# Spreading reciprocal softmax sums over the rows of a result: by a buffer off the chip in place of products with a selection matrix

## The reference, cut to what matters

```python
q = (x @ wq).reshape(b, n, heads, dh).transpose(0, 2, 1, 3)   # heads 20, dh 8
k = (ctx @ wk).reshape(b, j, heads, dh).transpose(0, 2, 1, 3)
v = (ctx @ wv).reshape(b, j, heads, dh).transpose(0, 2, 1, 3)
sim = jnp.einsum('bhid,bhjd->bhij', q, k) * dh ** (-0.5)
a = jax.nn.softmax(sim, axis=-1)
out = jnp.einsum('bhij,bhjd->bhid', a, v)
return out.transpose(0, 2, 1, 3).reshape(b, n, heads * dh) @ wo + bo
```

## Time and profile before

| | us |
|---|---|
| median of 3 runs | 3791.29 |
| lowest and highest run | 3786.4, 3798.77 |
| the profiled execution: its own time | 3797.55 |
| its span, first to last instruction | 3795.8 |
| mean granted TensorE clock over the span | 0.97 |
| PE busy in the span | 3625.6 (96%) |
| VectorE busy | 2304.9 (61%) |
| ScalarE busy | 2093.5 (55%) |
| GpSimd busy | 1249.9 (33%) |

### The profile page before, as it was taken

The page is one execution under the profiler, slowest core; times in us unless marked ns, Lnnn a source line. Parts: engine busy times, 40 slices in busy tenths (PEclk is TensorE's granted clock), DMA queues, the critical chain, the costliest instruction groups (busy, mean ns, idle before and its releaser), DMA issues. The chain is left out here.

```text
span 3795.8 us, 98161 instructions
## 1 busy us (share of the span) xinstructions
PE 3625.6 (96%) x37907; PEld 3133.8 (83%) x37907; DVE 2304.9 (61%) x3920; ACT 2093.5 (55%) x5164; POOL 1249.9 (33%) x1275
## 2 busy tenths in 40 slices
PE   5999999997997999999999999699999999999899
PEld 4777778876886888888898888588888888888788
DVE  2788866662454566666666666455555655556454
ACT  2777777773433655555555555355555555554333
POOL 4333333321442233333333332222222322222442
PEclk8999999995998999999999999899999999999899
DMA  4343333321001000000000000100000000000000
GB/s 109 90 102 101 92 82 91 87 77 50 5 0 44 1 1 0 0 0 0 0 0 0 0 0 1 25 3 2 2 2 1 2 2 2 2 1 1 16 21 24
DMA packets 99546, 98.72 MB, mean 26 GB/s; under 512 B 31248, under 2 KB 74128, under 8 KB 99344
## 3 DMA queue, kind: packets, MB, share of 16 engines
q1 hardware_dynamic: 94224, 94.50, 9.4%
q0 software_dynamic: 5120, 1.35, 0.2%
HBM read 20.76 MB, written 5.24 MB: 7 GB/s over the span
## 5 line engine op out<-in xcount | busy, mean ns | idle before, releaser
L1137 POOL TENSOR_TENSOR a_probs<-a_probs,a_rsums 128x1024 f32<-128x1024 f32 x160 | 303.6, 1898 | 750.6 <-DVE a_rsums L1235 750.6
L1157 ACT ACTIVATE a_probs<-a_scores_banks,a_negmax 128x128 f32<-128x128 f32 x1280 | 366.6, 376 | 297.6 <-DVE a_negmax L1223 297.6
L1137 POOL TENSOR_TENSOR c_probs<-c_probs,c_rsums 128x616 f32<-128x616 f32 x160 | 201.2, 1258 | 767.8 <-DVE c_rsums L1235 767.8
L702 ACT ACTIVATE s_probs<-s_scoresT_banks 128x1024 f32<-128x1024 f32 (+1 forms) x320 | 327.1, 1022 | 205.0 <-PE s_scoresT_banks L860 203.0
L1157 ACT ACTIVATE c_probs<-c_scores_banks,c_negmax 128x77 f32<-128x77 f32 x1280 | 312.1, 334 | 203.8 <-DVE c_negmax L1223 203.8
L777 DVE TENSOR_REDUCE s_negmax<-s_scores_banks 128x8 f32<-128x1024 f32 (+1 forms) x320 | 322.4, 1007 | 153.4 <-PE s_scores_banks L842 149.3
L1216 DVE COPY c_outT<-c_out_bank 128x512 f32<-128x512 f32 x160 | 110.7, 692 | 368.9 <-PE c_out_bank L1377 308.6
L1216 DVE COPY a_outT<-a_out_bank 128x512 f32<-128x512 f32 x160 | 110.7, 692 | 296.1 <-PE a_out_bank L1377 244.1
L1521 DVE SCALAR_TENSOR_TENSOR f_hidden<-f_value_bank,bias,f_gate 128x512 f32<-128x512 f32 x160 | 120.2, 751 | 263.1 <-ACT f_gate L1498 261.1
L665 POOL DMA_DIRECT2D s_q_stack<-s_shift x160 | 93.4, 584 | 523.3 <-ACT s_shift L725 517.4
L1498 ACT ACTIVATE f_gate<-f_gate_bank,bias 128x512 f32<-128x512 f32 x160 | 109.9, 687 | 257.3 <-PE f_value_bank L323 257.3
(11 more groups left out here) (288 smaller groups left out, 10613.9 us busy)
## 6 DMA issues: line engine op xcount, KB each, us to landing
s_q_stack<-s_q_compact SPq DMA_DIRECT2D x192, 160.0 KB, 3.2
s_k_stack<-s_k_compact SPq DMA_DIRECT2D x96, 160.0 KB, 3.6
s_out<-s_heads SPq DMA_DIRECT2D x128, 80.0 KB, 2.2
s_k_stack<-s_k_compact SPq DMA_DIRECT2D x96, 96.2 KB, 2.8
x_tokens<-in_x SPq DMA_DIRECT2D x16, 320.0 KB, 5.1
out_x<-x_tokens SPq DMA_DIRECT2D x16, 320.0 KB, 2.4
s_q_stack<-s_shift POOLq DMA_DIRECT2D x160, 8.0 KB, 2.5
s_ctx_in<-in_ctx SPq DMA_DIRECT2D x16, 115.5 KB
```

The source lines that it names most:

```text
L702: nc.scalar.activation(probs[i][0:NK, :, :], scoresT[0:NK, :, :], ACT.Exp).then_inc(s_exp, 1)
L1137: nc.gpsimd.tensor_tensor(probs[i][:], probs[i][:], rsums[(k - 1) % 2][:].unsqueeze(2).broadcast_to([P, UNIT, NK]), ALU.mult).then_inc(s_p ...
L1157: done = nc.scalar.activation(probs[i][:, h, :], scores[:, h // GROUP, h % GROUP * NK:(h % GROUP + 1) * NK], ACT.Exp, bias=negmax[k % 2][: ...
```

## The change

`select` and its products are gone. In unit 9 of period `n + 1` SyncE writes the reciprocal sums to a buffer in memory off the chip (`sums_out`, 40 KB). In unit 0 of period `n + 2` it waits until that has landed and reads them back by four transfers of 80 KB, each row of the buffer eight times, into `spread`, a tile of the shape of `out`. `sums` is now a part of `spread`, so the load of the next sums waits for the multiplies. VectorE multiplies the two halves of `out` by `spread` in two following units (`sums_at` now names units 2 and 3 in place of 1 and 3, and the multiply comes one unit behind), after a wait for all four transfers. PE's waits for `max_bank` between maxima and spread sums are gone.

```diff
-        sums = sb("sums", [HALF, P])
+        sums_out = nc.dram_tensor(f"{tag}_sums_out", (HALF * P,), F32, kind="Internal").ap()
+        spread = sb("spread", [HALF, 2, QUAD * P])
+        sums = spread[:, 0, 0:P]
...
-            return ((s - 1) // 2, n) if s in (1, 3) and live(n, TOTAL) else None
+            return (s - 2, n) if s in (2, 3) and live(n, TOTAL) else None
...
+                if s == 9 and live(prev, TOTAL):
+                    sp.wait_ge(s_rsums, prev + 1)
+                    sp.dma_start(sums_out.rearrange("(p n) -> p n", n=P), sums).then_inc(s_sums_out, 16)
+                if s == 0 and live(prev - 1, TOTAL):
+                    sp.wait_ge(s_sums_out, 16 * prev)
+                    if due(2 * (prev - 1)):
+                        sp.wait_ge(s_out, 2 * (prev - 1))
+                    for b in range(2):
+                        for j in range(2):
+                            source = sums_out[(2 * b + j) * 20 * P:(2 * b + j + 1) * 20 * P]
+                            sp.dma_start(spread[40 * j:40 * (j + 1), :, b * 2 * P:(b + 1) * 2 * P],
+                                         source.rearrange("(a g n) -> a g n", a=1, g=GROUPS).broadcast_to([8, GROUPS, 4 * P]))\
+                                .then_inc(s_spread, 16)
                 if s == 6 and live(prev, TOTAL):
                     sp.wait_ge(s_heads, GROUPS * (prev + 1))
-                    sp.dma_start(sums[:], heads[(local - 1) % 2][1:P:32, :, :]).then_inc(s_sums_in, 16)
+                    if due(prev):
+                        sp.wait_ge(s_out, 2 * prev)
+                    sp.dma_start(sums, heads[(local - 1) % 2][1:P:32, :, :]).then_inc(s_sums_in, 16)
...
-                spread = sums_at(k - 1)
-                if spread:
-                    half, n = spread
-                    dve.wait_ge(s_spread, 2 * n + half + 1)
+                scaled = sums_at(k - 1)
+                if scaled:
+                    half, n = scaled
                     if half == 0:
                         dve.wait_ge(s_out_in, 16 * OUT_DMAS * (n + 1))
-                    nc.vector.tensor_tensor(out[:, half, :], out[:, half, :], max_bank[0:HALF, :], ALU.mult).then_inc(s_out, 1)
+                        dve.wait_ge(s_spread, 16 * 4 * (n + 1))
+                    nc.vector.tensor_tensor(out[:, half, :], out[:, half, :], spread[:, half, :], ALU.mult).then_inc(s_out, 1)
...
-                    if g in (0, 1) and due(n - 1):
-                        pe.wait_ge(s_out, 2 * (n - 2) + g + 1)
...
-                spread = sums_at(k)
-                if spread:
-                    half, n = spread
-                    pe.wait_ge(s_rsums, n + 1)
-                    pe.wait_ge(s_shift, upto(5 * (n + 2) + half + 1 - 1, 5 * TOTAL))
-                    if n + 2 >= TOTAL:
-                        pe.wait_ge(s_out, 2 * n + half)
-                    for b in range(2):
-                        for r in range(2):
-                            col = (2 * b + r) * P
-                            last = nc.tensor.matmul(max_bank[0:HALF, col:col + P], m.select[0:HALF, b, 2 * half + r, :], sums[:],
-                                                    start=True, stop=True)
-                    last.then_inc(s_spread, 1)
...
-                link(nc.gpsimd.memset(m.select[:], 0.0))
-                for b in range(2):
-                    for x in range(4):
-                        place = m.select[0:D // 2, b, x, :].rearrange("p (j d g) -> p j d g", j=2, g=GROUPS)
-                        link(nc.gpsimd.affine_select(out=place, in_=place, compare_op=ALU.not_equal, fill=1.0, base=-(40 * b + x),
-                                                     pattern=[[-20, 2], [0, 8], [-4, GROUPS]], channel_multiplier=1))
```

More of the change, by code:

```diff
@@ L541, in attention_small @@
         s_rsums = sem("rsums_ready")
+        s_sums_out = sem("rsums_out")
         s_spread = sem("rsums_spread")
@@ L797, in step @@
                     dve.wait_ge(s_sums_in, 16 * quad_of(k))
-                    nc.vector.reciprocal(sums[:], sums[:]).then_inc(s_rsums, 1)
+                    nc.vector.reciprocal(sums, sums).then_inc(s_rsums, 1)
                 if s == 7 and live(ahead, TOTAL):
@@ L1594, in build @@
         m.minus_half = sb("minus_half", [P, QUAD])
-        m.select = sb("select", [P, 2, 4, D // 2])
         m.minus_low_row = sb("minus_low_row", [P, 1])
```

## The result

The changed kernel took 4066.15 us (median of 4 runs, 4050.41 to 4085.16), the kernel before 3789.06 in the same comparison (3786.40 to 3798.77): ratio 1.0728, 95% interval 1.0672 to 1.0784. The forecast was 3748, and the range ended at 3792. The profiled execution took 4075.63 us, against the 3797.55 shown of before.

A forecast was written before the change was run, and what follows sets the result against it. PE order was taken to set the time, VectorE following closely. Gains of 14.6 us in self, 21.1 in cross and 7.0 in the remaining periods made 43 us, from a median of 3791.29 to 3748; range 3730 to 3792.

The forecast's parts named there:

- The clock stays, as counted: End of the forecast's sum: 43 us gained, 3748 us, with the granted clock unchanged.
- PE has no idle time in those units without the sets either: Argument against the clock falling in cross quads, where two of ten units have sets but no unread products.
- its sum for cross: Cross quads: unit 5 starts at +10.62 against +12.13, gaining 1.51 us in each of 14, 21.1 us.
- The price of a fall: Quads at half clock: about 33 to 35 us instead of 25.25, 9 us more each, 45 us in all.
- up to five quads until a burst: Cross: a clock fall lasts at most until a burst in quads 18, 23 or 28, costing 45 us.
- The rival that the clock falls: Cross quads: without the sets PE works less and the clock drops; 3793 to 3835 us; chance 7%.
- The chain: SyncE's write, wait, four reads and VectorE's wait per quad: 6.0 us, bounds 5.5 to 7.6, worst 10.0.
- the rival of late transfers: Chain over about 8 us delays VectorE and PE; 3819 at 10.0 us; 10% slower, 20% for 7 to 9 us.
- the gain of undisturbed quads: Quads whose transfers land early: 1.38 us gained in self, 1.51 us in cross.
- the lock: Multiply from two SBUF tiles waits out GpSimd's running operation, then takes 0.57 us; rival without it 3731, 13%.
- the start, hidden as before: Kernel start: removing nine GpSimd operations on `select` changes nothing, as GpSimd idles 19.92 us afterwards.
- the signs of what to watch: Signs of error included VectorE idle 1 us or more before multiply 0 and clock 0.50 before 840 us.

The follow-up runs named there:

- run 5: Run 1 with GpSimd's shift transfer of unit 2 issued ahead of L422 and L424; 3765.41 us, ratio 0.9936.
- run 1: The changed kernel without the write and four reads, spread set once to 1.0, normalisation by the sums mostly left out; 3981.08 us.
- run 9: The changed kernel with GpSimd's shift transfer of unit 2 ahead of L422 and L424, both multiplies later in VectorE's unit 4; 3763.58 us, ratio 0.9927.
- run 10: Run 9 with reciprocal, write and reads early, in unit 8; 3755.00 us, ratio 0.9890.
- run 6: The changed kernel with reciprocal, write and reads early in unit 8, and GpSimd's shift transfer of unit 2 ahead of L422 and L424; 3881.73 us.
- run 4: The changed kernel with the reciprocal, write and reads moved early, into unit 8; 3985.64 us.
- run 11: Run 10 with four products that nobody reads per unit in quad 2 too; 3764.84 us, from 3745.30 to 4007.89 in five runs.
- run 2: The changed kernel with four unread products put back in units 1 and 3, ahead of the projection; 3819.04 us (3786.70 to 4063.57).
- run 7: The changed kernel with only GpSimd's shift transfer of unit 2 moved ahead of L422 and L424; 4021.05 us.
- run 8: The kernel before the change with 1.6 us of unread GpSimd work between L424 and the shift transfer of unit 2; 3873.31 us, ratio 1.0170.

## Why the prediction was wrong

**The step that failed** is the last sentence of the sum, "The clock stays, as counted", and the argument under its rival: "PE has no idle time in those units without the sets either". It took TensorE's order alone as the pace, and looked for what comes late only along the new chain. With the sets gone TensorE comes sooner to everything else that it waits for, and one of these, GpSimd's shift transfer behind the normalisation, had 4.1 us of cover in cross and then 2.1. The prediction had both ends of it in its sum for cross: L424 pushed to +9.25, and unit 5 at +10.62 (measured +10.49). Its scores take 0.64, so by these numbers the transfer behind L424 has 10.62 + 0.64 - 9.25 = 2.0 us, which it didn't set against the landings. In the kernel before, 8 of the 28 landings at this place, 5 of the 14 in cross, took more than 2.1 us from their issue (2.3 to 3.4); none made TensorE wait. Its trace had all of this, issue, landing and the use.

**The price of a fall** was wrong as well. A cross quad at half clock was put at 33 to 35 us from 102 records in 8 us, a stretch of longer products. It took 41.4 (44.0 in every fifth), 16 us more a quad and not 9. And "up to five quads until a burst" was no bound: of three bursts of fills at half clock one (in quad 23) was followed by a rise, and that held for 31 us. Of the fifteen periods that lost 221 us, twelve lost 15 to 17 each, 195 together. The rival that the clock falls, given 7%, had the end of the mechanism right, but the wrong beginning, missing work, which run 5 refutes for cross.

**The chain** took 6.0 us in the sum, within 5.5 to 7.6, with 10.0 as the worst. In the quads where VectorE waited it took 6.7 to 8.8. The write landed sooner than the 2.2 taken (1.5 at the median); the four reads were issued in 2.92 us, 0.73 each where at most 0.63 was assumed, and VectorE went on up to 4.1 us after the last issue ended (332.70 - 328.55). SyncE's own lateness was taken as up to 1.15 us, and was up to 2.4. So VectorE waited in 7 of 14 self quads, and in 4 of them TensorE stopped for more than 1 us: the rival of late transfers. Its price, 2.0 us a quad at 10.0, left the clock out: two periods around such a stop took 59.6, 61.3 and 62.8 us against 50.0 before, 10 to 13 us more.

**Right** were: the gain of undisturbed quads (self quads of 23.4 us in run 1, 23.6 in run 5 and 23.75 in the runs 9 and 10, 1.2 to 1.6 less than before, 1.38 forecast; cross 1.4 to 1.6 less, 1.51 forecast); the lock, with multiplies of 1.0 to 1.5 us amid GpSimd's work and 0.68 without; the start, hidden as before; and the signs of what to watch, waits before multiply 0 and the clock at 0.50 before 840 us. The sum, 43 us, is near what the edit is worth when hardly anything stops: run 10, with its new orders, gained 34. That the multiply waits for the whole GpSimd instruction is what the Trainium skill, "SBUF — State Buffer", SBUF: two separate sides, states; the trace agrees, with 1.52 us at 391.59, which ends 0.6 us after L424, and run 6 adds that it can be two instructions.

**Of a wait's size** the runs say this: in self the falls came behind stops of 1.7 to 3.4 us in the changed kernel, while stops of 0.68 us were passed, but in run 4 it fell behind stops of 0.64 and 0.68, at 177 and 330 us; in cross the falls came behind 1.86, 1.16, 1.16, 2.08, twice 2.39, 2.19 and 0.96 us, while 0.85 and 0.59 were passed. Where self passes into cross, stops of 0.5 to 0.6 us were passed in the kernel before and brought it down for 304 us in run 11. What exactly makes it fall is left open, as is why some landings of 8 KB take 1.7 us and others 4.7.

## What to carry to other kernels

When work is taken from the engine that sets the pace, list everything else that this engine waits for, and read for each how long before its use it is ready now: work that is removed was cover for all of them, not only for what replaces it. A transfer's cover has to be measured against its slowest landings (here 4 to 5 us beside a usual 1.8), since each quad draws again. And where the granted clock hangs on an unbroken stream, price a stop by what the clock does behind it (here 10 to 13 us in self, 16 us for each quad that follows in cross), not by its own microsecond.

## What the runs showed of the hardware

- Half clock is a trap of its own: in run 2 TensorE was 100% busy from 528 to 1139 us with all its fills, and the clock stayed at 0.50, though in the same quads it holds at 1.00 once it is there. From quad 17 on it rose only in quads with a burst, some 10 us after their start: in 4 of the 18 such quads that the traces of the changed kernel and of the runs 1, 2, 4, 6, 7, 8 and 11 show at half clock.
- A stop of 0.96 us could cost 80 us (run 8), one of 1.16 us 270 (run 2).
- A multiply out of two SBUF tiles that began while GpSimd issued a DMA (795.60 in run 6) waited for both GpSimd operations behind that, 2.89 us instead of 0.67: it got no turn between the two.
- The 8 KB shift transfer from GpSimd's queue landed in 1.7 to 4.7 us at the same place of the program; the 40 KB write off the chip from SyncE's in 1.5 to 3.2 in the changed kernel.
